# Reordering the on-chip buffers of a four-stage transformer kernel so that matrix operands start at multiples of 512 bytes

## What is computed

```python
x = L0_attn_q
x = x + _L0_attn_ref(_layernorm(x, axis=-1), L0_attn_w_qkv, L0_attn_w_dense)
x = x + _L0_ffn_ref(_layernorm(x, axis=-1), L0_ffn_A, L0_ffn_B, L0_ffn_Wr)
x = x + _L1_attn_ref(_layernorm(x, axis=-1), L1_attn_Wq, L1_attn_Wk, L1_attn_Wv, L1_attn_Wo, L1_attn_q_norm_w, L1_attn_k_norm_w)
x = x + _L1_ffn_ref(_layernorm(x, axis=-1), L1_ffn_gate_q, L1_ffn_gate_absmax, L1_ffn_up_q, L1_ffn_up_absmax, L1_ffn_down_q, L1_ffn_down_absmax)
```

## The kernel before

| buffers | before | after |
|---|---|---|
| `x`, `xt_hi`, `xt_lo`, `ident`, `xn` | 128 | 0 |
| `w_raw`, `w_hi`, `w_lo`, `wd_raw`, `wd_hi`, `wd_lo`, `tri` | 0 | 0 |
| `rel` | 128 | 0 |
| both attentions: `qt`, `kt`, `v`, `p0`, `p1`, `pt`, `ot` | 288 | 0 |
| first attention: `vt`, `lv_early`, `deq_early`, `code_early`, `absmax_early` | 416 | 0 |
| second attention: `k_tok` and `sq` | 416 | 0 |
| experts: `a_hi`, `a_lo`, `ranks`, `spread`, `gates`, `scores_t` | 288 | 0 |
| experts: `b_hi`, `b_lo` | 0 | 0 |
| experts: `a_raw`, `gated_hi`, `gated_lo` | 416 | 0 |
| last stage: `lv_late`, `deq_late`, `sg`, `hf`, `h_hi`, `h_lo` | 288 | 0 |
| last stage: `stage`, `code_late`, `absmax_late` | 384 | 0 |

## Time and profile before

### The profile page before, as it was taken

The page is one execution under the profiler, slowest core; times in us unless marked ns, Lnnn a source line. Parts: engine busy times, 40 slices in busy tenths (PEclk is TensorE's granted clock), DMA queues, the critical chain, the costliest instruction groups (busy, mean ns, idle before and its releaser), DMA issues.

```text
span 1725.9 us, 28815 instructions
## 1 busy us (share of the span) xinstructions
PE 1688.7 (98%) x9088; PEld 1415.8 (82%) x9088; DVE 1271.5 (74%) x2349; ACT 902.0 (52%) x2448; POOL 589.7 (34%) x714
## 2 busy tenths in 40 slices
PE   8999999999999998999999999999999997899999
PEld 7888888888888887987888888888888886688887
DVE  5788888888888787544777787778777779655555
ACT  2666566655565645323545555554445546554443
POOL 4325344343626254232213121222212103344442
PEclk9999999999999999999999999999999999999999
DMA  4122222221312221000101001100111002022111
GB/s 153 38 68 67 73 79 61 73 84 49 97 53 87 66 89 62 1 1 31 37 25 38 30 30 30 30 30 30 30 30 30 24 5 81 24 75 61 58 52 49
DMA packets 47711, 87.78 MB, mean 51 GB/s; under 512 B 6576, under 2 KB 6576, under 8 KB 47536
## 3 DMA queue, kind: packets, MB, share of 16 engines
q1 hardware_dynamic: 47664, 87.19, 16.3%
HBM read 77.73 MB, written 9.44 MB: 51 GB/s over the span
## 4 chain that ended last, share of the span: by engine, by line
PE 58%; DVE 4%; ACT 2%; POOL 1%; issue 1%; DMA 0%; DVEq 0%; ACTq 0%; POOLq 0%
PE ring L323 11%; PE ring L325 11%; PE ring L324 11%; PE scores L323 4%; PE scores L324 4%; PE scores L325 4%; PE turned L323 3%; PE turned L324 3%; PE turned L325 3%; PE scores L745 2%; PE turned L819 2%; PE turned L785 1%; PE turned L812 1%; ACT p L845 1%; PE turned L806 0%
## 5 line engine op out<-in xcount | busy, mean ns | idle before, releaser
L323 PE MATMUL ring<-xt_hi,w_lo 128*128 128x512 f32 x640 | 253.8, 397 | 2.4 <-issue 1.4
L325 PE MATMUL ring<-xt_hi,w_hi 128*128 128x512 f32 x640 | 253.3, 396 | 0.0
L324 PE MATMUL ring<-xt_lo,w_hi 128*128 128x512 f32 x640 | 253.2, 396 | 0.0
L588 POOL TENSOR_SCALAR w_hi<-w_raw 128x512 fp32r<-128x512 f32 x96 | 66.6, 693 | 501.8 <-PE turned L806 306.6
L323 PE MATMUL ring<-wd_hi,ot_lo 128*128 128x512 f32 x512 | 207.9, 406 | 10.2 <-DVE xt_lo L508 3.8
L836 ACT CAST pt_hi<-turned 128x512 fp32r<-128x512 f32 x192 | 100.7, 594 | 197.8 <-PE turned L812 193.5
L325 PE MATMUL ring<-wd_hi,ot_hi 128*128 128x512 f32 x512 | 202.9, 396 | 0.0
L324 PE MATMUL ring<-wd_lo,ot_hi 128*128 128x512 f32 x512 | 202.8, 396 | 0.0
L564 ACT ACTIVATE lv_early<-code_early 128x512 f32<-128x512 f32 x224 | 123.1, 640 | 54.5 <-POOL code_early L555 53.1
L323 PEld LDWEIGHTS ring<-xt_hi,w_lo 128*128 128x128 f32 x640 | 120.9, 189 | 28.7 <-issue 1.7
L325 PEld LDWEIGHTS ring<-xt_hi,w_hi 128*128 128x128 f32 x640 | 120.6, 188 | 28.9
(11 more groups left out here) (250 smaller groups left out, 4382.6 us busy)
## 6 DMA issues: line engine op xcount, KB each, us to landing
w_raw<-w_attn_dram SPq DMA_DIRECT2D x96, 256.0 KB, 3.1
wd_raw<-w_dense_dram SPq DMA_DIRECT2D x64, 256.0 KB, 2.7
code_early<-codes_dram SPq DMA_DIRECT2D x28, 256.0 KB, 2.8
absmax_early<-absmax_dram SPq DMA_DIRECT2D x56, 128.0 KB, 3.0
kept_dram<-deq_early SPq DMA_DIRECT2D x28, 256.0 KB, 2.0
stage<-kept_dram SPq DMA_DIRECT2D x28, 256.0 KB, 2.7
code_late<-codes_dram SPq DMA_DIRECT2D x14, 256.0 KB, 2.7
absmax_late<-absmax_dram SPq DMA_DIRECT2D x28, 128.0 KB, 2.9
```

Of the source, the lines that this page charges most:

```text
L323: nc.tensor.matmul(o, l_lo, r_hi, start=start, stop=False)
L324: nc.tensor.matmul(o, l_hi, r_lo, start=False, stop=False)
L325: return nc.tensor.matmul(o, l_hi, r_hi, start=False, stop=stop)
```

## The change

Only places in memory change. The small statistics buffers go ahead of `x` (384 bytes, which brings `x` to 1536); `rel` goes ahead of `ones`; small buffers go behind the large ones in each scope; `norm_cols`, `grec` and two fillers change size so that what follows starts at a multiple of 512. The instructions, their order, their shapes and the semaphores are the same; `grec` is now used through its first two columns.

```diff
+        bn = sb("bn", [P, NT, 6])
+        mv = sb("mv", [P, NT, 2])
+        var_eps = sb("var_eps", [P, NT])
+        rstd = sb("rstd", [P, NT])
+        newton = sb("newton", [P, NT])
+        shift = sb("shift", [P, NT])
         x = sb("x", [P, NT, D])
         xt_hi = sb("xt_hi", [P, DC, TOK], F32R)
         xt_lo = sb("xt_lo", [P, DC, TOK], F32R)
         ident = sb("ident", [P, P])
         xn = sb("xn", [P, 2, D])
-        bn = sb("bn", [P, NT, 6])
-        mv = sb("mv", [P, NT, 2])
-        var_eps = sb("var_eps", [P, NT])
-        rstd = sb("rstd", [P, NT])
-        newton = sb("newton", [P, NT])
-        shift = sb("shift", [P, NT])
...
         tri = sb("tri", [P, P])
+        rel = sb("rel", [P, SEQ + P])
         ones = sb("ones", [P, 32])
-        rel = sb("rel", [P, SEQ + P])
         slopes = sb("slopes", [P, GROUPS * HEADS])
-        norm_cols = sb("norm_cols", [P, 3])
+        norm_cols = sb("norm_cols", [P, 64])
...
-            negmax = sb(f"negmax{layer}", [P, 2, HEADS], F32, scope)
-            bias = sb(f"bias{layer}", [P, 2, HEADS], F32, scope)
-            sums = sb(f"sums{layer}", [P, 2, HEADS], F32, scope)
-            rsum = sb(f"rsum{layer}", [P, 2, HEADS], F32, scope)
             if rms:
                 k_tok = sb("k_tok", [P, HALF // P, HD], F32, scope)
+                sq = sb("sq", [P, HEADS, HALF], F32, scope)
+                k_square = sb("k_square", [P, 2, HD], F32, scope)
                 k_sum = sb("k_sum", [P, HALF // P], F32, scope)
-                k_square = sb("k_square", [P, 2, HD], F32, scope)
...
-                sq = sb("sq", [P, HEADS, HALF], F32, scope)
             if not rms:
...
+            negmax = sb(f"negmax{layer}", [P, 2, HEADS], F32, scope)
+            bias = sb(f"bias{layer}", [P, 2, HEADS], F32, scope)
+            sums = sb(f"sums{layer}", [P, 2, HEADS], F32, scope)
+            rsum = sb(f"rsum{layer}", [P, 2, HEADS], F32, scope)
...
+            gate = sb("gate", [P, 2, EXPERTS], F32, scope)
             top = sb("top", [P, 2, 2, 8], F32, scope)
             top_neg = sb("top_neg", [P, 2], F32, scope)
-            gate = sb("gate", [P, 2, EXPERTS], F32, scope)
             gsum = sb("gsum", [P, 2], F32, scope)
-            grec = sb("grec", [P, 2], F32, scope)
+            grec = sb("grec", [P, 80], F32, scope)
             b_hi = sb("b_hi", [P, EC, D], F32R, scope)
             b_lo = sb("b_lo", [P, EC, D], F32R, scope)
-            sb("behind_attention", [P, 744], F32, scope)
+            sb("behind_attention", [P, 640], F32, scope)
...
-            sb("up_to_the_second_attention", [P, 14488], F32, scope)
+            sb("up_to_the_second_attention", [P, 14592], F32, scope)
```

More of the change, by code:

```diff
@@ L267, in psum @@
             return ctx.enter_context(nc.psum_tensor(name, shape, F32))
[L270 to L274, removed]
         bn = sb("bn", [P, NT, 6])
@@ L280, in build @@
         shift = sb("shift", [P, NT])
+        x = sb("x", [P, NT, D])
+        xt_hi = sb("xt_hi", [P, DC, TOK], F32R)
+        xt_lo = sb("xt_lo", [P, DC, TOK], F32R)
+        ident = sb("ident", [P, P])
+        xn = sb("xn", [P, 2, D])
         scores1 = psum("scores1", [P, HEADS, SEQ])
@@ L1488, in router @@
                 dve_link(nc.vector.tensor_reduce(gsum[:, :], gate[:, :, :], AX.X, ALU.add))
-                dve_link(nc.vector.reciprocal(grec[:, :], gsum[:, :]))
-                dve_link(nc.vector.tensor_scalar(grec[:, :], grec[:, :], LORA_SCALE, None, ALU.mult))
+                dve_link(nc.vector.reciprocal(grec[:, 0:2], gsum[:, :]))
+                dve_link(nc.vector.tensor_scalar(grec[:, 0:2], grec[:, 0:2], LORA_SCALE, None, ALU.mult))
                 nc.vector.tensor_tensor(gate[:, :, :], gate[:, :, :],
-                                        grec[:, :].unsqueeze(2).to_broadcast([P, 2, EXPERTS]),
+                                        grec[:, 0:2].unsqueeze(2).to_broadcast([P, 2, EXPERTS]),
                                         ALU.mult).then_inc(s_gates, 1)
```

## The result

The changed kernel takes 1709.46 us (median of 4 runs, 1708.3 to 1709.63) against 1724.78 us for the kernel before; the ratio is 0.9907, with a 95% interval of 0.9894 to 0.9921. It is faster, by 15.3 us where 36 were forecast. The time lies inside the stated range, in the region of its smaller cases. The span of the profiled execution fell from 1725.9 to 1707.9 us, 18.0 us. That is more than the medians show because the profiled execution of the kernel before had a low mean granted clock, 0.995: in the later comparison of run 10 that kernel took 1727.5 to 1727.8 us at 0.995 and 1722.53 us at 0.999.

What follows compares the result with a forecast made beforehand. TensorE's matmul stream was taken to bound the kernel: matmul count times start-to-start distance. Gains summed to 36.7 us, less 1 us for waits, giving 1689 us as forecast, range 1680 to 1713.

Steps and rivals of the forecast that it cites:

- Query, key and value tiles, gate and up: Attention tiles and last stage: 2592 matmuls of 512 columns, each 5.5 ns quicker once both operands are aligned, 14.3 us.
- Output products: Attention output products: 1536 matmuls at 232.6 ns, each 5.4 ns quicker, 8.3 us.
- `pv`: Attention `pv` products, both operands at 288: 576 matmuls at 231.1 ns, each 3.9 ns quicker, 2.2 us.
- down: Down products: 336 matmuls, each 5.4 ns quicker, 1.8 us.
- expert outputs: Experts' output products of batches 1 and 3: 96 matmuls, each 6.4 ns quicker like batches 0 and 2, 0.6 us.
- Scores and `kv`: 1536 matmuls of 256 columns, each losing the same fixed 5.5 ns as 512-column ones, 8.4 us; lower bound 0.
- ranks: 384 matmuls with stationary rows of 4352 bytes, only every other one aligned, so half of 5.5 ns each: 1.1 us.
- Given back in waits: Joints between stages where TensorE waits for VectorE: quicker matmuls only lengthen the wait, 1 us off the gain.
- Only the stationary side: Rival: moving operand's place doesn't count, tiles' 14.3 us fall away, 1704 us; shares 0.18 with a middle course.
- Nothing: Rival: placement in another sense made batches 0 and 2 quick, main streams stay, 1725 us; chance 0.13.
- the slower one: Rival: all buffers at one remainder make reads collide, 6.4 ns per slow 512-column matmul, +33 us, 1758 us; chance 0.05.
- How the two operands lie to each other: Rival: relative place counts, streams end at `pv`'s pace, 1718 us; middle course 1704 to 1712; 0.18 shared with one-sided.

Runs made afterwards that it cites:

- run 10: Kernel before, no buffer moved, with only ScalarE's first four code lines of batch 3 moved behind pv in the first attention: 1722.08 us, ratio 0.9983.
- experiment 3: Kernel before with only the statistics buffers put ahead of x, so x, xt, ident and xn go to remainder 0: 1714.18 us, ratio 0.9931.
- experiment 4: Changed kernel with the six statistics buffers back behind xn, everything else left at remainder 0: 1719.63 us, ratio 0.9963.
- experiment 9: Separate matmul streams, stationary at 0, moving at twelve places, plus short streams behind transposes: 512 columns took 226.7 ns at 240, 233.4 at 16 bytes beyond.
- experiment 2: Separate matmul streams at remainder 0, varying widths, stationary columns and busy neighbours: 256 columns took 120.0 ns with 128 stationary columns, 113.5 with 64.
- experiment 1: Separate matmul streams pairing seven moving with seven stationary places: at 512 columns, 226.7 to 227.9 ns when remainders agree modulo 256, mostly 232.2 to 234.3 otherwise.
- experiment 8: Changed kernel with kt moved to remainder 32 and a to 224, beside their partners at 0: 1705.44 us, ratio 0.9884.
- experiment 7: Changed kernel with ScalarE's first four code lines of batch 3 moved behind pv in the first attention: 1702.5 us, ratio 0.9872.
- experiment 5: Changed kernel with a 288-byte buffer ahead of x, putting every operand at remainder 288 of 512: 1708.9 us, ratio 0.9904.
- experiment 6: Changed kernel with 256 bytes ahead of w_raw, so x, xt, ident and xn stay at 0 and the rest goes to 256: 1707.44 us, ratio 0.9897.

## Why the prediction was right in sign and wrong in size

**What bounds the kernel, and the distance as its measure: right.** Every gain is a shorter distance between matmuls at an unchanged count.

**Query, key and value tiles, gate and up (14.3 us forecast).** 13.9 us came, in the distances that changed by no more than 30 ns: 10.1 in the attentions' tiles, 3.8 in the last stage. The moving side, inferred only, was real (experiments 3 and 4).

**Output products (8.3), `pv` (2.2), down (1.8), expert outputs (0.6).** They brought 6.3, 0.9, 2.2 and 0.6 us, 10.0 in place of 12.9. The last two are long settled streams. The output products are streams of 12 and 24, many of them behind products of another kind, and pay for settling with about six slow distances (experiment 9). The forecast took the pace of a stream of 48 for them. `pv` is another matter: its operands had a common place before the change, so it had no pace of its own to gain, and the 0.9 us came because 29 of its streams stand behind tiles that got quicker.

**Scores and `kv` (8.4), ranks (1.1).** This term was the largest error: -0.1 and 0.1 us in place of 9.5. The step that failed is "a column costs the same in all streams, and what misplacement adds is a fixed 5.5 ns". The two equations fitted (113.6 = 232.7 - 119.1, and twice that 227.2) by coincidence. At 256 columns the distance is near the floor that goes with 128 stationary columns, 111 ns (experiment 2), the common place is there no advantage but, with 120 ns, among the slowest (experiments 1 and 9), and a place 32 bytes off gives the small gain that was there to take (experiment 8). The scores had both operands at 288 and so the common place already; `kv` and the ranks got it (a row of 4352 bytes is 17 times 256, so every row of the ranks did, not every other one), and `kv` became slower by it, 118.3 to 120.0 ns. The bound of 0 was in the text, and the value should have been nearer to it as long as no aligned 256-column row existed.

**Given back in waits (1 us).** This is the second step that failed: 8.5 us were given back. Luck hid part of it, as the profiled execution had one stretch at the 1.2 GHz level less than the one before, and 2.6 us came back by that. The forecast looked at VectorE's busy share (84%) for cover. The share can't show a chain across engines: VectorE's and GpSimd's work on the codes, ScalarE's code lines, the exponentials, then `ot_hi` behind them in ScalarE's queue and `ot_lo` behind that. From the code lines on it took 7.44 us before and after; its end came 0.10 us earlier where TensorE came 0.46 us earlier, and 0.36 us a turn were lost, 2.5 us in all. In the earlier trace rows only the largest line was read; this wait was in the same list with 3.3 us in 9 times. Experiments 7 and 10 show it: taking the cause away was worth 3 us before the change and 5 to 6 after it. The other 6 us of grown waits were not tested by a run; 2.6 of them, behind the scores, are again waits for VectorE.

**The rivals.** "Only the stationary side" is refuted. "Nothing" is refuted, and so is the slower one. "How the two operands lie to each other" was the true mechanism, with the wrong reason against it: the quick batches being quicker than `pv` was put down to alignment, when it was the length of the stream. For the tiles, the output products and the last stage both mechanisms foretell the same, since multiples of 512 have also a common place; experiments 1, 5 and 6 tell them apart, and so do `pv` and the scores, which had a common place before. That the measured 1709.5 us lies in the 1704 to 1712 us that the forecast gave to a middle course of this rival is luck: the streams didn't end at a pace between, most ended at 227 ns.

**The sum, corrected.** 13.9 + 6.3 + 0.9 + 2.2 + 0.6 - 0.1 + 0.1 = 23.9 us from the distances (23.8 before rounding), less 8.5 us from waits, plus 2.6 us from the clock, is the 17.9 us of span. The forecast had 36.7 less 1.

## What to carry to other kernels

In a stream of float32r matmuls, look at starts and not at durations, and give the moving and the stationary operand the same remainder modulo 256 bytes: with 512 columns that was worth 6.5 ns of 233 each, wherever the common place lay; with 256 columns and 128 stationary ones it was worth nothing. Don't extend a per-instruction gain to another width without a row of that width: another floor may lie just beneath. And before summing up savings on the bounding engine, look for waits that recur every turn, however small, and follow what they wait for through the other engines to its start: what TensorE saves beside such a chain is not saved.

## What the runs showed of the hardware

- A float32r matmul of 512 columns costs 226.7 ns from start to start if moving and stationary operand agree modulo 256 bytes or the moving one is 16 bytes short of it, about 229 if it is 48 or 64 bytes further on, 232 to 234 otherwise (experiments 1 and 9). Why, the traces don't say: that the read for the running matmul and that for the next one's stationary operand get into each other's way fits with it but wasn't shown. The Trainium skill ("TensorE: Matmul & The Clock Gate", section "Step-by-step: what each phase is for") says that loading the next weights takes no read bandwidth from the running matmul, since the two have ports of their own; the 6.5 ns between pairs that differ in place alone (experiment 1) don't fit with full independence, and the measurement decides.
- Where the operands agree, a stream settles into 227 ns within three to ten matmuls; where they don't, it never does (experiment 9).
- With 128 stationary columns a matmul took at least about 111 ns; with 64 it took 60 ns at 128 moving columns (experiment 2).
- VectorE, ScalarE, GpSimd and DMAs beside the stream changed nothing, aligned or not (experiment 2).
